# Telling finished matmuls by drains: a graph network's edge loop on TensorE

## The reference

```python
# layer 0: a 16x16 matrix for every edge, made from its 16 attributes
ew = (efeat @ W_e + b_e).reshape(E, in_f, out_f)
msg = jnp.einsum('ei,eio->eo', feat[src], ew)
summed = jax.ops.segment_sum(msg, dst, num_segments=N)
neigh = summed / jnp.maximum(cnt, 1.0)[:, None]
# layer 1: a 16x16 matrix for each of 8 edge types, then a GRU step
m = jax.ops.segment_sum(jnp.einsum('emh,eh->em', A[etype], h[src]), dst, N)
# around both
x = layernorm(x + layer(x, ...))
```

## Time and profile before

| | us |
|---|---|
| median of three runs | 6261.09 |
| lowest, highest | 6250.47, 6273.0 |
| profiled execution, from first to last instruction | 6277.1 |
| TensorE matmuls busy (PE) | 5108.7 (81%) |
| VectorE, ScalarE, GpSimd busy | 3968.6, 4007.9, 3566.7 |

### The profile page before, as it was taken

How to read it: one execution, slowest core, us unless ns; L and a number is a source line. 1 busy time by engine, 2 the same in 40 slices (tenths; PEclk the granted TensorE clock), 3 DMA queues, 4 the chain that set the end, 5 groups by cost and what they waited for, 6 DMA issues and landing times.

```text
span 6277.1 us, 131101 instructions
## 1 busy us (share of the span) xinstructions
PE 5108.7 (81%) x39898; PEld 4605.9 (73%) x39899; DVE 3968.6 (63%) x4891; ACT 4007.9 (64%) x5658; POOL 3566.7 (57%) x3745
## 2 busy tenths in 40 slices
PE   6888888888888888888777877778887778877777
PEld 5777777777777777777577777777777777777777
DVE  6666666676666666666655555555555555555556
ACT  6666666666666666666556666666666666666665
POOL 6555555555555555555555555555555555555554
PEclk9999999999999999999889989899999888988998
DMA  3111111111111111111111111111111111111110
GB/s 63 27 29 28 28 29 28 29 27 30 27 29 27 28 29 28 29 27 28 21 21 22 20 21 20 20 20 21 21 21 21 20 20 22 20 21 20 21 21 14
DMA packets 336894, 156.46 MB, mean 25 GB/s; under 512 B 196220, under 2 KB 335963, under 8 KB 336723
## 3 DMA queue, kind: packets, MB, share of 16 engines
q1 hardware_dynamic: 218224, 124.50, 8.9%
q0 software_dynamic: 118464, 30.56, 7.0%
q10 hardware_dynamic: 160, 0.80, 0.1%
HBM read 152.87 MB, written 2.66 MB: 25 GB/s over the span
## 4 chain that ended last, share of the span: by engine, by line
PE 54%; issue 15%; ACT 14%; another core or an unknown queue 12%; DVE 4%; ACTq 1%; DVEq 0%; POOL 0%; DMA 0%; SPq 0%; POOLq 0%
PE psN L782 43%; PE psM L819 9%; ACT dist L576 7%; ACT pick L584 6%; DVE cand L982 1%; DVE z L1013 1%; ACTq L329 1%; PE psTR L800 1%; DVE z L988 0%; ACT sumT L560 0%; ACT psD L599 0%; PE psTR L790 0%; PE psTR L803 0%; ACTq L575 0%
## 5 line engine op out<-in xcount | busy, mean ns | idle before, releaser
L782 PE MATMUL psN<-table_hi,pick 128*128 128x320 f32 x12740 | 4038.1, 332 | 919.2 <-ACT pick L584 538.2
L782 PE MATMUL psN<-table_lo,pick 128*128 128x320 f32 x12740 | 3909.2, 321 | 13.8 <-issue 13.0
L782 PEld LDWEIGHTS psN<-table_hi,pick 128*128 128x128 f32 x12740 | 2575.5, 202 | 1125.4 <-ACT pick L584 585.0
L782 PEld LDWEIGHTS psN<-table_lo,pick 128*128 128x128 f32 x12740 | 2579.4, 202 | 19.0 <-issue 17.8
L504 POOL DMA_INDIRECT z<-h_rows,idx x1817 | 1737.9, 956 | 1379.2 <-PE psN L782 619.9
L504 POOL DMA_INDIRECT z<-in_x,idx x1885 | 1802.4, 956 | 1264.3 <-issue 496.3
L982 DVE TENSOR_TENSOR cand<-psN,grp_hot 128x640 f32<-128x640 f32 (+1 forms) x1306 | 1043.8, 805 | 1964.7 <-PE psN L782 1273.2
L584 ACT ACTIVATE pick<-dist,one 128x640 fp32r<-128x640 bf16 (+1 forms) x2485 | 1978.6, 835 | 412.3 <-remote 248.0
L576 ACT ACTIVATE dist<-src_mod,neg_node 128x640 bf16<-128x640 uint16 (+1 forms) x2485 | 1970.5, 831 | 33.0 <-ACT pick L584 15.7
L1013 DVE TENSOR_TENSOR z<-psD,z 128x2048 f32<-128x2048 f32 (+1 forms) x750 | 1366.9, 1823 | 55.0 <-issue 33.2
L603 ACT COPY sumS<-psM 128x273 f32<-128x273 f32 (+1 forms) x250 | 81.9, 328 | 1697.4 <-PE psM L819 1258.5
(11 more groups left out here) (109 smaller groups left out, 759.4 us busy)
## 6 DMA issues: line engine op xcount, KB each, us to landing
src_mod<-src_mod_rows SPq DMA_DIRECT2D x434, 160.0 KB
z<-in_x,idx POOLq DMA_INDIRECT x1885
z<-h_rows,idx POOLq DMA_INDIRECT x1817
eab<-in_edge_attr SPq DMA_DIRECT2D x125, 200.0 KB
src_mod<-src_mod_rows SPq DMA_DIRECT2D x63, 192.0 KB
idx<-in_src SPq DMA_DIRECT2D x250, 12.5 KB
dstb<-in_dst SPq DMA_DIRECT2D x250, 14.0 KB
grp<-src_grp SPq DMA_DIRECT2D x249, 5.5 KB
```

What stands on the lines that cost most here:

```text
L782: mm = pe.matmul(rows[:, :, 0:cells.shape[2]], pick[j][:, c, at:at + P], cells, start=(i == 0 and part == 0), stop=(i == TC - 1 and part = ...
```

## The change

The four increments leave their matmuls. In their place TensorE's sequencer gets a drain instruction behind the group, and the drain carries the increment. For columns there is no drain behind each: `tells` is true for the second column of each pair and for the last of each half, so the drains stand behind columns 1, 3, 4, 5, 7 and 9 (and 10, where there are 11), and each adds the number of columns since the one before. Whoever waits for a column in between now waits for the next told one.

```diff
+        def tells(k, buf, t):
+            return t % 2 == 1 or t + 1 in HCUT[k][buf]
...
-                    mm.then_inc(l["picked"], 1)
+                    told = [u for u in range(H[k][buf]) if tells(k, buf, u)]
+                    if t in told:
+                        pe.drain().then_inc(l["picked"], t - max([u for u in told if u < t], default=-1))
...
-                        pe.transpose(psT[:, 2 * P:3 * P], sumS[:, 2 * P:3 * P], ident[:]).then_inc(tp, 1)
+                        pe.transpose(psT[:, 2 * P:3 * P], sumS[:, 2 * P:3 * P], ident[:])
...
-                        pe.transpose(psT[:, 0:P], sumS[:, 0:P], ident[:]).then_inc(tp, 1)
+                        pe.transpose(psT[:, 0:P], sumS[:, 0:P], ident[:])
+                    pe.drain().then_inc(tp, 1)
...
-                        pe.matmul(psR[:, 0:P], W0[:, 2, :], sumT[:, 2, :], start=False, stop=True).then_inc(res, 1)
+                        pe.matmul(psR[:, 0:P], W0[:, 2, :], sumT[:, 2, :], start=False, stop=True)
...
-                        pe.matmul(psR[:, 0:P], A1[:], sumT[:, 0, :], start=True, stop=True).then_inc(res, 1)
+                        pe.matmul(psR[:, 0:P], A1[:], sumT[:, 0, :], start=True, stop=True)
+                    pe.drain().then_inc(res, 1)
...
-                    mm.then_inc(mm_done, 1)
+                    pe.drain().then_inc(mm_done, 1)
```

## The result

The changed kernel takes 7039.98 us (median, 7036.97 to 7045.36) against 6261.09: ratio 1.1253, 95% interval [1.1223, 1.1283]. It is slower by 779 us; I had forecast 261 us faster, with a range that ended at 6600. Its profiled execution spans 7043.6 us.

The account below looks back on a forecast made before the run. Bound by TensorE in most of a block, otherwise by waits, mostly for its matmuls' late tells. 6277 + 716 (drains) - 843 (prompt tells) - 127 (clock) = 6023 us profiled, forecast as 6000 us, range 5650 to 6600.

Parts of the forecast that it names:

- What the prompt tells give: TensorE's idle time in both layers: drains tell promptly, so 843 of 1063 us come back, 220 us stay.
- the first rival: Matmul completions themselves are late, so drains come as late and nothing comes back: 6850 us, chance 0.15.
- What the drains cost: Stops of TensorE's stream at 2304 drains: 2054 at 0.33 us, 250 at 0.15 us, together 716 us more.
- The restart: Behind a drain on TensorE: the next matmul is let go 0.06 us after the last one's end.
- the second rival: TensorE's restart behind drains is dearer, slow feeding being laid bare: 6570 us, turning point 0.42 us a drain, chance 0.17.
- The clock: TensorE's granted clock in layer 1 rises from 0.90 to 0.95, saving 127 us; nothing in layer 0.
- Coarser tells: Columns 0, 2, 6 and 8 told with the next one: GpSimd's waits end 1.45 us later, costing nothing.

Follow-up runs that it names:

- Experiment 1: The kernel before, all matmuls telling as before, plus a silent drain wherever the change has a telling one: 6911.43 us, ratio 1.0895.
- experiment 6: Both kernels unchanged on a chip with prompt completions: the kernel before 4941.98 us, the changed kernel 5978.66 us, ratio 1.2101.
- experiment 4: Changed kernel with layer 0's block sum behind column 3, not 4: 7109.27 us; changed kernel with a drain behind every column (994 more): 6948.25 us.

## Why the prediction was wrong

**The step that failed is "What the prompt tells give", 843 us.** It read "the increment came 4.0 us after the modelled end" as the lateness of one messenger, and took it that with the sequencer's own increment "the lateness goes". But a drain waits for the same late notice of completion, or for a later one: this is the first rival (0.15, 6850 us), which had left open whether the array or its bookkeeping is late. Experiment 1 shows it at the single event, 0.033 us between the two tells. What the step rested on was the timeline's end of a matmul, and the legend of the page says that these ends are modelled. The argument against the rival was that the next matmuls start 0.03 us behind the transposes and run on through the 4.0 us. It doesn't bear on a drain: a matmul starts without the notice of the one before, while a drain ended with that notice or behind it (experiment 1). The rule that I had named on the rival's side (the Trainium skill, PSUM — Partial Sum Buffer, Engine vs sequencer instructions: an engine's update fires on completion) agrees with the traces in so far as increment and drain come together. That the tell at 3040.97 was the moment at which the work was done is not shown; the tells 0.11 us apart speak against reading each tell so. The size of the 843 us was no fancy: where completions are prompt, TensorE idles 66 + 163 = 229 us in its two layers, 834 less than in the earlier trace rows (there the clock differs as well). What was wrong is that a drain could fetch them.

The times add up as follows. From the one profiled execution to the other the span grows by 7043.6 - 6277.1 = 766 us; TensorE's busy time grows by 5275.0 - 5108.7 = 166 us and its idle time by 600. On the chip with prompt completions the span grows by 5976.6 - 4938.8 = 1038 us: busy by 5064.0 - 4648.1 = 416 us, idle by 622 us. So the idle time grows by nearly the same amount with late completions as without: of the 843 us nothing came back on balance. The two differ in busy time, by 250 us, and that fits the clock, which rose in the one and could not in the other.

**What the drains cost: 716 us were forecast, 1038 are measured** where completions are prompt (0.45 us each, net of what fell into idle time, and with the coarser tells). The count was right, 2304. The restart was mis-sized: 0.20 us from the drain's end to the next matmul instead of 0.06, with the sequencer's work on its next wait in between. The larger waits behind the result and at a block's boundary were not in the sum at all. From the drain's end to the next matmul there are 800 us over the 2304 drains of experiment 6, 0.35 us on the mean. This is the second rival's mechanism ("the restart is dearer", turning point 0.42 us); I had looked for it in the earlier trace rows, and it lay in the scalar instructions between columns, which the page doesn't count as busy. Both rivals held in part: nothing came back, and a drain is dearer than the 0.33 us with which the first came to 6850 us. By kind: 413 us for 750 drains at sums, transposes and results (0.55 each), 664 us for 1554 at columns (0.43 each), together 1077 and so close to the whole that the parts hardly overlap. The instruction itself is a small part: a second drain on the idle array costs (6150.77 - 5978.66) / 2304 = 0.075 us (two chips, on which the kernel before agrees to 1 us).

**The clock: 127 us forecast, up to 250 found** (the difference of the busy times above; no run isolates it), right in kind. The records of the granted clock fit: it was at its lower level for 997 us before and for 515 us after, and half of the difference, what the lower level costs a busy TensorE, is an estimated 241 us. In experiment 6 it was there for 37 and 44 us. At one place before, it fell in a long stretch without a matmul: the stretches of the kernel before around,

```profile
5008.00:5014.20 6.20, 0.00 (x0) 0.00 (x0) 0.00 (x0) 1.62 (x3) 3.55 (x4) 0.63 0.22 31
5014.20:5020.00 5.80, 4.77 (x18) 4.78 (x19) 4.00 (x4) 1.74 (x2) 1.91 (x2) 0.51 0.06 7
```

show 0.63 of the full clock in a stretch where no matmul starts, and 0.51, close to the level of 1.2 GHz, in the one behind it. But it isn't the lower clock that makes completions late: from 3036.6 to 3041.0, around, the granted clock is 1.00,

```profile
3036.60:3041.00 4.40, 1.80 (x13) 1.54 (x12) 2.55 (x4) 1.24 (x3) 2.90 (x4) 1.00 0.07 6
```

and the transposes are 4.0 us late all the same. Of the 594 late drains of the changed kernel, 555 have no stretch at the lower level from 5 us ahead of their last matmul to their end.

**Coarser tells** were forecast at nothing and cost 0.5%. The forecast with the measured terms: 6277 + 1038 - 0 - 250 + 0 = 7065 us, where 7044 was profiled; the coarser tells' 29 us are inside the 1038. The 250 us are themselves a difference of the two pairs, so what this sum tests is only that the idle time grew alike in both (600 and 622 us). Whether recording makes the lateness was not tried; experiment 6 was recorded in the same way and has none. The kernels that come out under the kernel before, 0.9955 and 0.9971, leave work out; no version tried beats it with all its work done.

## What to carry to other kernels

A matmul's end in the trace is a model. Before a "late tell" is counted as time to be won, make both tells in one kernel, here a silent drain behind a telling matmul: if they come together, a drain is no faster, whatever makes both late. A drain of TensorE's sequencer in a stream of dense matmuls costs some 0.5 us here, and it lays bare every scalar instruction that a full queue had hidden, so price the sequencer's code between the groups first. And look at whether the kernel's waits are its own: the two layers of the same program had 1063 us of idle TensorE in one comparison and 229 us in another, on another chip.

## What the runs showed of the hardware

- The kernel before took 6261, 6342 and 6246 us in three comparisons, with completions up to microseconds late and a mean clock of 0.91 to 0.93, and 4942, 4941 and 4943 us in three others with a clock of 0.996 and none late. Each comparison kept to one chip, and the last five are on five different ones. What sets the two kinds apart isn't known. The program is the same. But the three with late completions were also the first three in time, so chip and time are not told apart.
- Where completions were late, they were mostly late at the same places of a block (556 of 594 late drains at five places), and moved when the order of the work was changed (experiment 4). With 994 more stops the lateness of all drains fell from 859 to 474 us. Columns of 1.44 us of work were told 0.11 us apart.
- So the price of the change was 12.5% where completions were late and the clock had room to rise, and 21.0% where they were prompt. Where the kernel before was faster, the change cost more, in us (1038 against 779) as in share.
